# Identity products on TensorE at four borders between stages of a two-layer perceiver kernel

## What is computed

```python
x = x + L0_xattn(ctx, layernorm(x))   # 16 heads of 64, keys from context and latents
x = x + L0_attn(layernorm(x))         # self attention, 16 heads of 16, q and k normed
x = x + L0_ffn(layernorm(x))          # 64 experts, top 8, and a shared branch
x = x + L1_xattn(layernorm(x), ctx)   # 16 heads of 64
x = x + L1_attn(layernorm(x))         # heads of 16 mapped to 32, rotary, causal
x = x + L1_ffn(layernorm(x))          # three products, tanh
```

```python
q, k, v = split(x @ c_attn_w.T + c_attn_b)
q_lat, k_lat, v_lat = q @ q2l_w.T + q2l_b, k @ kv2l_w.T + kv2l_b, v @ kv2l_w.T + kv2l_b
q_lat, k_lat = rotate(q_lat), rotate(k_lat)
att = softmax(causal((q_lat @ wqk_w.T + wqk_b) @ k_lat.T * 32 ** -0.5))
y = (att @ v_lat) @ l2o_w.T + l2o_b
```

## Time and profile before

| | us |
|---|---|
| median of 3 runs | 2562.22 |
| the three runs | 2559.76, 2562.22, 2567.51 |
| the profiled execution | 2569.55 |
| its span on the core | 2567.8 |
| TensorE matmul busy | 2430.7 (95%) |
| VectorE busy | 1697.7 (66%) |
| POOL busy | 1452.0 (57%) |
| ScalarE busy | 1280.4 (50%) |
| mean granted TensorE clock | 0.981 |

### The profile page before, as it was taken

How to read it: one execution, slowest core, us unless ns; L and a number is a source line. 1 busy time by engine, 2 the same in 40 slices (tenths; PEclk the granted TensorE clock), 3 DMA queues, 4 the chain that set the end, 5 groups by cost and what they waited for, 6 DMA issues and landing times. The chain is left out here.

```text
span 2567.8 us, 64424 instructions
## 1 busy us (share of the span) xinstructions
PE 2430.7 (95%) x24562; PEld 1895.0 (74%) x24577; DVE 1697.7 (66%) x4004; ACT 1280.4 (50%) x2972; POOL 1452.0 (57%) x1641
## 2 busy tenths in 40 slices
PE   7999999999999999999798997799999999998997
PEld 3557787878788888886566586688888888885665
DVE  6877877777777777774666733666665666553665
ACT  4656656565656565654442233354445444543433
POOL 6867757575757576765762255666446643332233
PEclk9999999999999999999998999999999999999998
DMA  5341212121212111111005188533224422210001
GB/s 195 138 146 40 66 32 51 31 51 31 51 33 48 35 46 36 45 30 35 8 4 187 58 257 276 168 104 97 81 67 102 96 70 67 72 46 15 3 3 36
DMA packets 224819, 190.05 MB, mean 74 GB/s; under 512 B 89217, under 2 KB 212674, under 8 KB 224514
## 3 DMA queue, kind: packets, MB, share of 16 engines
q1 hardware_dynamic: 208994, 153.92, 20.4%
q0 software_dynamic: 9216, 27.28, 4.6%
q10 hardware_dynamic: 6304, 4.72, 0.6%
HBM read 151.53 MB, written 34.31 MB: 72 GB/s over the span
## 5 line engine op out<-in xcount | busy, mean ns | idle before, releaser
L295 POOL TENSOR_TENSOR rk<-ss,neg_half 128x32 f32<-128x32 f32 x64 | 348.0, 5437 | 248.3 <-DVE ss L277 248.3
L1868 PE MATMUL banks<-rowsT,qk 128*128 128x257 f32 x1024 | 243.1, 380 | 0.9 <-ACT qk L1788 0.9
L328 ACT ACTIVATE ksq<-kT 128x512 f32<-128x512 f32 x256 | 161.1, 630 | 163.1 <-DVE kT L271 163.0
L271 DVE COPY kT<-banks 128x512 f32<-128x512 f32 x256 | 176.9, 692 | 61.7 <-PE banks L382 56.9
L382 PE MATMUL banks<-x_hi,wk_hi 128*128 128x256 f32 x1024 | 213.4, 289 | 1.9 <-DVE kT L271 1.7
L1868 PEld LDWEIGHTS banks<-rowsT,qk 128*128 128x128 f32 x1024 | 189.2, 190 | 27.4 <-ACT qk L1788 1.2
L382 PE MATMUL banks<-x_hi,wk_lo 128*128 128x256 f32 x1024 | 206.8, 284 | 0.0
L382 PE MATMUL banks<-x_lo,wk_hi 128*128 128x256 f32 x1024 | 205.7, 282 | 0.1
L1275 ACT ACTIVATE score<-score,ntop 128x289 f32<-128x289 f32 x256 | 135.4, 530 | 113.1 <-DVE ntop L1139 112.9
L1677 POOL DMA_INDIRECT parts<-scratch_expert,address x128 | 132.3, 1034 | 90.3 <-DVE residual L1571 45.6
L1706 POOL CAST r_hi<-diff 128x512 fp32r<-128x512 f32 x64 | 43.1, 674 | 243.1 <-PE banks L1894 242.3
(11 more groups left out here) (369 smaller groups left out, 6509.5 us busy)
## 6 DMA issues: line engine op xcount, KB each, us to landing
rowsT<-in_ctxT SPq DMA_DIRECT2D x64, 257.0 KB, 2.9
wgu<-in_expert_gu SPq DMA_DIRECT2D x64, 256.0 KB, 3.9
rows<-in_ctx SPq DMA_DIRECT2D x64, 256.0 KB, 3.2
raw<-in_ctx SPq DMA_DIRECT2D x61, 256.0 KB, 2.8
scratch_qT<-qT SPq DMA_DIRECT2D x16, 512.0 KB, 2.6
scratch_kT<-kT SPq DMA_DIRECT2D x16, 512.0 KB, 3.0
q<-scratch_qT SPq DMA_DIRECT2D x64, 128.0 KB
kT<-scratch_kT SPq DMA_DIRECT2D x64, 128.0 KB
```

The source lines that it names most:

```text
L271: nc.vector.tensor_copy(m.kT[:, k, 2 * i:2 * i + 2, 0:ROWS], banks[i % 2].rearrange("p (a r) -> p a r", a=2)).then_inc(s.kT, 1)
L295: nc.gpsimd.tensor_tensor(m.rk[:], m.ss[:], kit.neg_half[:, 0:KF * H], ALU.pow).then_inc(s.rk, 1)
L328: nc.scalar.activation(m.ksq[:, 2 * i:2 * i + 2, :], m.kT[:, k, 2 * i:2 * i + 2, 0:ROWS], ACT.Square).then_inc(s.ksq, 1)
L1868: mm = nc.tensor.matmul(score[h][:, c - h * HALF, 0:CTX], m.qk[:, f, j, c * BT:(c + 1) * BT, :].rearrange("p h q -> p (h q)"), m.rowsT[:, ...
```

## The change

`Kit` gets a helper that multiplies the 128 x 128 fp32 identity by itself into the first 128 columns of a bank. Nothing reads these columns; the real products that use the bank later start it anew. It is called with bank 7 at four places, always on TensorE: 40 times ahead of `rotary.products`; 11 times ahead of the first step of "sa0" and 8 times ahead of that of "sa1"; and 18 times in step -2 of "sa0", ahead of `queries_keys_T` of tile 0. No wait is added and none removed; no other engine's program changes.

```diff
+    def keep_warm(self, bank, count):
+
+        for _ in range(count):
+            self.nc.tensor.matmul(self.psum(bank)[:, 0:P], self.ident[:], self.ident[:], start=True, stop=True)
...
+                kit.keep_warm(7, 40)
                 rotary.products(pe)
...
                 def step(n, has):
                     if has(1):
                         scores(n + 1)
+                    if n == -2 and not rotary:
+                        kit.keep_warm(7, 18)
                     if has(2):
                         queries_keys_T(n + 2, has(3))
...
                 if rotary:
                     pe.wait_ge(s.one, 1)
                 pe.wait_ge(weights.loaded, weights.count)
+                kit.keep_warm(7, 8 if rotary else 11)
                 steps(step)
```

## The result

| | before | changed |
|---|---|---|
| median of 7 runs, us | 2562.83 | 2578.10 |
| lowest and highest | 2559.76, 2567.51 | 2569.01, 2585.66 |
| the profiled execution | 2569.55 | 2571.07 |
| its span on the core | 2567.8 | 2569.2 |

The changed kernel is slower: the ratio is 1.0059, 95% interval 1.0043 to 1.0074, or 15 us. The prediction said 2563.0 in a range of 2556 to 2571, and it was wrong: it had a loss of 0.8 us. The profiled execution is one of the changed kernel's lowest, 7 us under its median, as that of before is 7 us over its own, so the two spans side by side hide most of the difference.

What follows compares the result with a forecast made beforehand. TensorE was taken to bound the kernel, busy for 95% of the span at nearly full clock. Terms of -1.0, +1.2, 0.0 and +0.6 summed to +0.8 us on a median of 2562.22: 2563.0 us, range 2556 to 2571.

Steps and rivals of the forecast that it cites:

- The border terms: Effects at the four places of the added products: -1.0, +1.2, 0.0 and +0.6, in sum +0.8 us.
- Forty products: Ahead of the rotary products: mostly hidden by the transfers, first group faster behind them; -1.0 us, between -1.85 and 0.0.
- The eleven: Ahead of sa0: transposes start later, full clock gives part back; +1.2 us, between +0.4 and +2.0.
- The eighteen: Step -2 of sa0: hidden by POOL's power, VectorE still waits for POOL; 0 us, at worst +0.7.
- The eight: Ahead of sa1: work starts later, full clock gives part back; +0.6 us, between 0.0 and +1.2.
- The rivals: Clock never falls: -1.45 (0.18); step -2 passes gain: -3.5 (0.08); all half clock lost: 7.0 faster (0.05); additions slow: +10.6 (0.06).
- Rival 4: At the blocks' beginnings: additions run at half clock and stand in front of real work; +10.6 us, 2572.8; chance 0.06.
- effects that no row shows: Anywhere in the kernel: chance of 0.03 left for effects outside the forecast and its four rivals; no size given.
- within 0.3%: Whole kernel: time within 7.7 us of before, chance 0.90; faster by over 0.3% 0.05, slower 0.05.
- theory A: From the experiments: the count of added instructions moves the places where TensorE's stream is refilled, and with them the stops.

Runs made afterwards that it cites:

- e10: Kernel before with only the forty identity products ahead of the rotary products, on a third chip: ratio 0.9962.
- e4: Kernel before with only the forty identity products ahead of the rotary products, on a first chip: ratio 0.9973.
- e6: Kernel before with forty one-column products ahead of the rotary products, on a second chip: ratio 1.0000.
- e11: Kernel before with forty one-column products ahead of the rotary products, on a third chip: ratio 0.9962.
- e1: Kernel before with 29 one-column products at the program's start and 48 ahead of the rotary products: ratio 1.0059 (2580.83 us).
- e2: Changed kernel with 35 more one-column products at the start and 16 ahead of the experts, against the kernel before: ratio 1.0012.
- e12: The changed kernel once more, unaltered, on a third chip, against the kernel before: ratio 1.0050.
- e8: Kernel before with 64 one-column products at the program's start: ratio 0.9998.
- e5: Kernel before with 24 one-column products, then the forty identity products, ahead of the rotary products: ratio 1.0035.
- e7: Kernel before with sa0's eleven and eighteen identity products, and 35 one-column products in step 10 of sa0: ratio 1.0017.

## Why the prediction was wrong

*The border terms held.* Forty products: predicted 10.75 us, with one half-clock stretch inside; measured 10.80, and 11.15 in e10. From the first group's start to the second's took 2.25 us (2.2 predicted, 3.92 before), and from the border to the first copy it was 17.76 us in place of 18.93: -1.17, where I took -1.0. This is one execution: the same stretch was 0.8 us shorter than before in e10 and 0.2 longer in e4. The eleven: +0.24, my bound was +0.4 and I took +1.2, since the clock didn't fall at all there. Without them the path from VectorE's `xl` to its first `ss` varies: 6.88 us in six traces, 5.18 in two (e6, e11) and 7.68 in e1; with them it was 7.12 in all five. So the eleven buy steadiness and no time. The eighteen: 0, as taken; POOL's power holds VectorE's `qk`, as the earlier trace rows said. The eight: +0.05 (I took +0.6), and +1.37 in e2 and in e12, just beyond my bound of +1.2; without any of the eight this path was 6.65 us in two traces (e8, e10) and 9.59 in e5, so no single trace prices it. The measured terms sum to -0.9 us, where I had +0.8.

*The rivals.* None of the four is what happened. Rival 4 had the right sign, but its mechanism, the forty outlasting their cover with four slow ones, did not decide: by the same working 10.80 us is eight slow ones, and they gained. Its cousin, the forty broken up by stops, showed in e5 only.

*The step that failed* is the list of terms. I added what lies at the four spots and left 0.03 "for effects that no row shows". The four spots came out at -0.9 us as measured, and the whole at +15, so some 16 us lay in a term that the sum put at nothing; e1, with none of the products at the four spots, has the same ratio of 1.0059. There was a row: the page of before lists queue 8, kind instruction, 199 packets and 3.26 MB, and its waits of TensorE in the two self attentions name "issue" for 24 us, three of them over 2 us in straight runs. I had read neither, because the queue's share of the DMA engines is 0.5% and because I looked for waits at the borders alone. From them the term could have been bounded: 24 us of stops whose places depend on the instruction count can move by some us up or down, so any change by a number of TensorE instructions that is no multiple of 256 carries an uncertainty of about 10 us either way. The runs gave -10 us (160 in sa1) to +9 us (116, by sa0's products alone), and +15 for the whole change. Such a term would not have told the sign, but it would have made 0.90 for "within 0.3%" untenable.

*The half clock elsewhere.* I counted the clock of the four spots and let the rest of the program stand. It did not: over the whole span the clock was 0.981 in both profiled executions. At the borders it rose (sa0's first 20 us from 0.75 to 1.00, the 15 us of the rotary products from 0.54 to 0.89, the 4 us at sa1's beginning from 0.57 to 1.00), which is 24 us less at half clock; from 1334 to 1392 us it fell from 0.88 to 0.71, which is 20 us more, and the rest went in other places.

**A version that was faster in three comparisons of four** is the kernel before with forty products, full or of one column, ahead of the rotary products alone: 0.9973 and 0.9962 of its time on two chips with the full ones, 0.9962 and 1.0000 with the small ones. It gains by the shift, and by theory A the next edit of TensorE's program ahead of it can take the gain away; that was not run.

## What to carry to other kernels

When an edit adds or removes instructions on an engine that later runs long blocks of very short ones, count them and take the rest over 256: the edit also moves the places at which the stream is refilled, and a control with the same count of one-column products in an idle place tells that effect from the edit's own. Before crediting a small gain or loss to an edit, look for "issue" idle inside straight runs and compare the instruction number at which it falls. Look also at whether one kernel measured twice, on two chips, agrees with itself before reading differences of some tenths of a percent between chips. And waking an idle engine is worth only what the next late engine lets through: here -1.2 us at one border, nothing or a loss at three.

## What the runs showed of the hardware that was not expected

- TensorE's instructions arrive in packets of 16.4 KB, one per 256 instructions. In runs of 32 x 32 fp32 products, 256 instructions in 1.29 us, TensorE stops for 0.2 to 2.9 us, at most once per packet; the stops of over 1 us end 2.2 to 2.9 us after the packet's transfer starts. In sa0 of both kernels a packet begins 0.5 to 3.2 us after TensorE has passed the place before, but for the last one before the border (8.0 us). In sa0's last tiles most stops were longer at pair 85 to 104 of a block of 128 (1.82 to 2.90 us, but 0.30 to 0.57 in one block of each trace, and 0.39 once in another) than at 15 to 34 (0.19 to 2.05), and with the former the packets began later behind the place before. Why they did, no run here shows.
- The place of the stops is the same to within a pair in every trace with the same shift, on three chips; the granted clock behind them is not.
- A product of one column by one row costs 53 ns of TensorE, loads included.
- TensorE can stop for "issue" at other places too: in e5 it did so nine times for 7.4 us in all, inside products of 0.23 us each, with no packet of the instruction queue under way. Why is open.
- Along the long stops of sa0's end the clock of the changed kernel was at half for 27 us, with TensorE busy without a gap in the last of it (5.00 of the 5 us from 1385 to 1390). In e7, with two stops of 1.37 and 1.76 us there, it was at half for nearly 24 us too, so the late stops are not what it takes. At the borders before, three half-clock stretches lasted 3.3 to 3.4 us under steady work.
